# Reordering the first third of a three-layer CIN kernel: W1 and x of chunk 1 ahead of the pairs' x, chunk 5's right fields loaded, and one x1 product ahead of the A products

## The chip, the cores and the metric

One core of one Trainium2 chip. The metric is the device time of one execution in microseconds (us); the median of several runs is compared.

## What is computed

The reference applies three compressed-interaction layers to x, which has 64 samples, 32 fields and 64 embedding positions. Cut to what matters:

```python
X0 = inputs.reshape(-1, 32, 64)
Xi = X0
for W, b in ((W1, b1), (W2, b2), (W3, b3)):
    Wr = W.reshape(128, 32, Xi.shape[1])
    Xi = jnp.einsum('bhd,bmd,ohm->bod', X0, Xi, Wr) + b[None, :, None]
    pools.append(Xi.sum(axis=-1))
y = concatenate(pools, -1) @ fc_W.T + fc_b
```

Only a number for each sample is wanted of layers 2 and 3, so the kernel folds their weights with fc_W. What stays is one full product with W1 (called **x1**), one product of the same size with a small matrix **A** that the kernel itself works out from W3, W2 and fc_W, and their elementwise product, summed.

## The kernel before

**Tiling.** The 4096 columns (64 positions by 64 samples) are cut into 8 chunks of 512. The features of a chunk are products of a left and a right field: four 128-row tiles, in two halves of two tiles, and a small tile of 96 rows for pairs that the four do not hold. Each float32 factor is split in two parts, high and low (`xs`, `feat`, `w1_hi`/`w1_lo`, `a_hi`/`a_lo`), so that three fast matrix products replace an exact one.

**One chunk.** `split_x(c)`: ACT rounds x to the high part, POOL (L259) subtracts for the low part. `pick_right(c, half)` (L567): two PE matmuls select the right fields into PSUM. `mult(c, half)` (L461): DVE multiplies left by right. `hi(c, half)` (L366): ACT rounds. `lo(c)`: DVE (L484) subtracts for half 0, POOL (L266) for half 1. For chunks from `PICKED` (6) on, the right fields are not picked by PE but loaded as 1 MB by `load_right(c)` (L185) into `r_in`, and DVE multiplies two SBUF tiles. `x1_product(c)` is 13 PE matmuls (`x1_hi`, `x1_lo` for each half, then `x1_tail`) into one of two PSUM banks; ACT empties it by `save_x1(c)` (L372), and a product for chunk c waits for `save_x1(c - 2)`. `a_product(c)` is 14 matmuls of the same kind with A.

**The A chain.** `v_part(0..3)` (L639) multiply W3 by a window of fc_W into `vt_ps`; ACT copies it, PE transposes it (L700), ACT writes `v_st`. `a_round(0..3)` (L665) multiply that with W2; ACT empties each round by `save_a(t)` (L377) into `at_sb`; SP stores each round with three DMAs to a scratch tensor in HBM (L205), and once all twelve have landed (`a_out`) SP (L233, L237, L239) and ACT (L432) load them back, rearranged, into `f1` and `f2`. DVE adds the two (L530, L532; `f_sum`), ACT rounds to `a_hi`, DVE subtracts to `a_lo`. Only then can `a_product(0)` run.

**The pairs' tile.** `x16` is loaded (L385), multiplied (L514), split (`z16_hi` on ACT, `z16_lo` on POOL, L309), spread by PE (`spread16(0)`, `spread16(1)`, L652) and copied by ACT (`save_zz`) to `zz`, which `x1_tail` and `a_product` read.

**What sets the order.** Every engine runs one instruction stream in the order of the code, and semaphores order the engines among each other; the orders are written out by hand: SP from L208, POOL from L275, ACT from L385, DVE from L507, PE from L678. The loads stand in one SP queue: x 0, W1, x 1, W3 in four parts with x 2 between, x 3, W2 in four parts with x 4 between, the rest of W1, x 5, x 6. ACT's queue has only x16 and the small vectors. `keep_clock` (L562) issues matmuls whose result nobody reads. POOL's wait list is in order too: what stands behind `split_x(5)` waits until ACT has rounded x 5. Four lines show a coupling that the prediction uses; on ACT, behind A's twelve stores, stand the loads and then the next chunk:

```python
act.wait_ge(a_out, A_OUT)
for j in range(J):
    act.dma_start(f2[...], ...).then_inc(f_main_in, 16)
hi(5, 0); hi(5, 1)
```

Behind these are the copy to `v_rep` (L438), `save_x1(2)`, the wait for `f_sum`, `a_hi`, and `save_x1(3)` (L440 to L443).

## Time and profile before

| | before |
|---|---|
| median of 3 runs | 81.9 us (81.87 to 82.09) |
| the profiled execution | 81.76 us |
| its span | 80.0 us |
| mean granted TensorE clock | 0.998 |
| PE / PEld / DVE / ACT / POOL busy | 72.5 / 51.6 / 46.6 / 34.6 / 49.8 us |
| PE / POOL / ACT / DVE / DMA on the chain that ended last | 77% / 5% / 3% / 3% / 7% |
| moved by DMA | 12.01 MB |

The span is what lies between the first and the last instruction; 1.76 us of the execution lie around it. A busy share says how long an engine worked, not that the end waited for it; the chain of waits, followed back from the last instruction, says that. PEld is the loading of weights beside the matmuls. Times in the rows are microseconds from the span's start.

### The profile page before, as it was taken

Reading aid. Unit: us, or ns where it says so; the run is one execution under the profiler, and the core shown is the slowest. Engines: PE = TensorE matmul, PEld = TensorE weight load, DVE = VectorE, ACT = ScalarE, POOL = GpSimd, SP = SyncE. Lnnn points to the kernel's source line nnn. Section 1 sums busy time; section 2 is a strip of 40 time slices with the busy share of each in tenths; the row PEclk is TensorE's granted clock in tenths of the full one; section 3 lists DMA queues with packets and bytes.
Section 4 is the critical chain, followed back from the end, with each engine's and each line's share of the span. In section 5 each row is a group of like instructions: output and inputs, shape, how many; then the busy total and the mean of one; then the engine's idle time right before and its main releaser. Section 6 shows DMA issues by size and latency. Waiting matters only on the chain.

```text
span 80.0 us, 1146 instructions
## 1 busy us (share of the span) xinstructions
PE 72.5 (91%) x372; PEld 51.6 (65%) x372; DVE 46.6 (58%) x44; ACT 34.6 (43%) x51; POOL 49.8 (62%) x49
## 2 busy tenths in 40 slices
PE   4969499978999669999999999999999999999970
PEld 1315177843445356888888888888888888886840
DVE  1058699686859999289699819992003003213541
ACT  1833997279948956890864700552300300000000
POOL 4989846999994399738079989809955004162400
PEclk9999999999999999999999999999999999999999
DMA  1899999999995615439997000000000000000000
GB/s 22 250 362 266 368 370 351 381 386 390 372 330 163 189 37 135 117 69 381 394 335 307 12 4 0 4 0 0 0 0 0 0 0 0 0 8 0 0 0 0
DMA packets 7529, 12.01 MB, mean 150 GB/s; under 512 B 835, under 2 KB 3971, under 8 KB 7267
## 3 DMA queue, kind: packets, MB, share of 16 engines
q1 hardware_dynamic: 6915, 11.16, 40.8%
q10 hardware_dynamic: 608, 0.77, 3.1%
q8 instruction: 3, 0.05, 0.2%
q14 instruction: 3, 0.02, 0.1%
HBM read 10.88 MB, written 1.05 MB: 149 GB/s over the span
## 4 chain that ended last, share of the span: by engine, by line
PE 77%; DMA 7%; POOL 5%; ACT 3%; DVE 2%; issue 2%; SPq 1%; POOLq 0%; DVEq 0%
PE a_ps L581 28%; PE x_ps L581 25%; DMA w_sb<-w 7%; PE z_ps L575 6%; PE a_ps L674 5%; PE a_ps L636 2%; PE x_ps L609 2%; PE a_ps L635 2%; PE a_ps L647 2%; POOL w_sb L305 2%; POOL z_lo L309 2%; POOL xs L259 2%; DVE r_in L477 2%; PE a_ps L661 1%; PE x_ps L749 1%
## 5 line engine op out<-in xcount | busy, mean ns | idle before, releaser
L266 POOL TENSOR_TENSOR feat<-r_in,feat 128x1024 fp32r<-128x1024 f32 x8 | 19.2, 2403 | 4.6 <-ACT feat L360 4.1
L581 PE MATMUL x_ps<-feat,w_hi 128*128 128x512 f32 x64 | 19.0, 395 | 0.0
L581 PE MATMUL a_ps<-feat,a_hi 128*128 128x512 f32 x64 | 16.2, 395 | 0.0
L259 POOL TENSOR_TENSOR xs<-x_in,xs 32x512 fp32r<-32x512 f32 x7 | 10.8, 1548 | 7.6 <-ACT xs L360 7.3
L504 DVE SCALAR_TENSOR_TENSOR x<-a_ps,vec,x 128x512 f32<-128x512 f32 x7 | 5.2, 746 | 17.7 <-PE a_ps L636 17.7
L273 POOL TENSOR_TENSOR x<-x 128x512 f32<-128x512 f32 x6 | 7.8, 1292 | 10.7 <-DVE x L504 10.5
L581 PEld LDWEIGHTS x_ps<-feat,w_hi 128*128 128x128 f32 x64 | 11.9, 188 | 3.4 <-issue 0.8
L581 PEld LDWEIGHTS a_ps<-feat,a_hi 128*128 128x128 f32 x64 | 11.9, 188 | 2.7
L484 DVE TENSOR_TENSOR feat<-z_ps,feat 128x1024 fp32r<-128x1024 f32 x8 | 9.8, 1220 | 3.5 <-ACT feat L360 3.4
L360 ACT ACTIVATE feat<-z_ps 128x1024 fp32r<-128x1024 f32 x8 | 8.2, 1022 | 5.8 <-DVE z_ps L477 5.8
L581 PE MATMUL x_ps<-feat,w_lo 128*128 128x512 f32 x32 | 9.8, 391 | 0.0
L575 PE MATMUL z_ps<-xs,pick 128*128 128x512 f32 x24 | 7.6, 417 | 2.4 <-POOL xs L259 1.4
L374 ACT ACTIVATE x<-x_ps,vec 128x512 f32<-128x512 f32 x8 | 5.4, 682 | 9.5 <-PE x_ps L609 9.5
L360 ACT ACTIVATE feat<-r_in 128x1024 fp32r<-128x1024 f32 x8 | 8.4, 1055 | 2.2 <-DVE r_in L477 2.2
L581 PE MATMUL a_ps<-feat,a_lo 128*128 128x512 f32 x32 | 8.6, 390 | 0.0
L477 DVE TENSOR_TENSOR r_in<-x_in,z_ps 128x1024 f32<-128x1024 f32 x6 | 7.3, 1217 | 1.3 <-issue 1.3
L477 DVE TENSOR_TENSOR z_ps<-x_in,z_ps 128x1024 f32<-128x1024 f32 x6 | 7.4, 1226 | 1.2 <-PE z_ps L575 1.2
L575 PEld LDWEIGHTS z_ps<-xs,pick 128*128 128x128 f32 x24 | 4.0, 188 | 5.7 <-POOL xs L259 2.5
L581 PEld LDWEIGHTS x_ps<-feat,w_lo 128*128 128x128 f32 x32 | 6.0, 188 | 1.4
L581 PEld LDWEIGHTS a_ps<-feat,a_lo 128*128 128x128 f32 x32 | 6.0, 188 | 1.3
L565 PE MATMUL x_ps<-at_sb 128*128 128x512 bf16 x17 | 5.6, 494 | 1.2 <-DVE at_sb L507 1.2
L360 ACT ACTIVATE xs<-x_in 128x512 fp32r<-128x512 f32 x8 | 5.0, 628 | 2.6 <-DMA x_in<-xl 2.5
(76 smaller groups left out, 74.7 us busy)
## 6 DMA issues: line engine op xcount, KB each, us to landing
w_sb<-w SPq DMA_DIRECT2D x9, 512.0 KB, 8.7
x_in<-xl SPq DMA_DIRECT2D x8, 256.0 KB, 7.3
r_in<-xr SPq DMA_DIRECT2D x2, 1024.0 KB, 6.0
a_by_fields<-at_sb SPq DMA_DIRECT2D x8, 96.0 KB, 2.1
x<-x ACTq DMA_DIRECT2D x1, 512.0 KB, 4.5
x<-x SPq DMA_DIRECT2D x1, 512.0 KB, 6.2
w_sb<-w SPq DMA_DIRECT2D x1, 256.0 KB, 11.6
a_by_fields<-at_sb SPq DMA_DIRECT2D x4, 64.0 KB, 2.1
```

The lines of the kernel that those rows point to most:

```text
L259: nc.gpsimd.tensor_tensor(xs[rows, c, :], x_in[rows, c % X_BUFS, :], xs[rows, c, :].bitcast(f32), ALU.subtract).then_inc(xs_lo, 1)
L266: nc.gpsimd.tensor_tensor(feat[:, c, 1, of_half(1), :], z_of(c, 1), feat[:, c, 0, of_half(1), :].bitcast(f32), ALU.subtract).then_inc(lo_d ...
L273: nc.gpsimd.tensor_tensor(x1[:, 0, :], x1[:, 0, :], x1[:, c, :], ALU.add).then_inc(acc_done, 1)
L360: return nc.scalar.activation(dst, src, ACT.Copy)
L374: nc.scalar.activation(x1[:, c, :], x1_ps[c % 2][:, :], ACT.Identity, bias=vec[:, 0:1]).then_inc(x1_saved, 1)
L477: nc.vector.tensor_tensor(z_of(c, half), left, right, ALU.mult).then_inc(z_done, 1)
L484: nc.vector.tensor_tensor(feat[:, c, 1, of_half(0), :], z_of(c, 0), feat[:, c, 0, of_half(0), :].bitcast(f32), ALU.subtract).then_inc(lo_d ...
L504: nc.vector.scalar_tensor_tensor(out=x1[:, c, :], in0=a_ps[:, c % 2, :], scalar=vec[:, 3:4], in1=x1[:, c, :], op0=ALU.add, op1=ALU.mult).t ...
L565: nc.tensor.matmul(x1_ps[1][:, :], blank[:, 0:M], blank[:, 0:N], start=True, stop=True)
L575: last = nc.tensor.matmul(field_bank(c, half)[:, k, :], pick[:, half * PER_HALF + k, :], xs[:, c, :], start=True, stop=True)
L581: nc.tensor.matmul(bank, weights[:, k, :], feat[:, c, part, k, :], start=(start and k == 0), stop=False)
L674: last = nc.tensor.matmul(a_ps[64 * g:64 * g + 64, t % 2, :], v_st[:, :], w2_sb[:, first:first + N], start=True, stop=True)
```

## The change

- **Loads.** x16 leaves ACT's queue and stands in SP's behind W3's second part, so that nothing but x 0 stands before W1 and x 1. x 2, x 3 and x 4 each move one 512 KB part forward, W1's rest moves ahead of W2. `PICKED` is 5: chunk 5's right fields are loaded (`load_right(5)`, behind x 5) and `pick_right(5, ...)`, four matmuls, goes. The buffers of `r_in` go by `right_buf(c)`. `load_right(6)` and `load_right(7)` stand in SP's queue where those of 6 and 7 stood; that of 6 now waits for chunk 5's last use.
- **POOL.** W1's sum stands first, then `split_x(1)`; the small copies and `ident` come behind it; `lo(0)` moves ahead of `split_x(2)`; `z16_lo` moves behind `lo(1)`; the sum of W1's rest goes to DVE.
- **ACT.** `z16_hi` moves behind `hi(1, 1)`, the `v_st` copies behind `hi(2, 1)`, `save_zz(0)` behind them; the four `save_a` stand among `hi(3, 0)` to `hi(4, 1)`; `save_zz(1)` moves ahead of the wait for `a_out`.
- **DVE.** x16's product moves behind chunk 1, `rest_sum` stands between the two halves of chunk 3.
- **PE.** `spread16(0)` moves behind `pick_right(3, 0)`; all four `v_part`, both halves of `x1_hi(1)`, the transpose and the rounds of A take new places; `x1_product(5)` stands ahead of q and of the A products, `x1_product(6)` ahead of `a_product(2)`.

```diff
@@ -25,7 +25,7 @@
...
-PICKED = 6
+PICKED = 5
 X_BUFS = 4
@@ -129,6 +129,7 @@
...
         w_sum, w_hi_done, w_lo_done = sem("w_sum"), sem("w_hi_done"), sem("w_lo_done")
+        w_rest_sum = sem("w_rest_sum")
         f_sum, a_hi_done, a_lo_done = sem("f_sum"), sem("a_hi_done"), sem("a_lo_done")
@@ -164,13 +165,17 @@
...
+        def right_buf(c):
+
+            return (c - PICKED) % 2
+
         def z_of(c, half):
...
                 return r_in[:, 1, of_half(c % 2), :]
-            return r_in[:, c % 2, of_half(1), :]
+            return r_in[:, right_buf(c), of_half(1), :]
@@ -183,12 +188,12 @@
...
             def load_right(c):
-                if c % 2 == 0:
+                if c == PICKED:
                     sp.wait_ge(spread_done, 3)
                 else:
-                    sp.wait_ge(hi_done, count(PICKED - 1, 1))
-                    sp.wait_ge(lo_done[1], PICKED)
-                sp.dma_start(r_in[:, c % 2, :, :], xr[c]).then_inc(r_here[c % 2], 16)
+                    sp.wait_ge(hi_done, count(c - 1 if c == PICKED + 1 else c - 2, 1))
+                    sp.wait_ge(lo_done[1], c if c == PICKED + 1 else c - 1)
+                sp.dma_start(r_in[:, right_buf(c), :, :], xr[c]).then_inc(r_here[right_buf(c)], 16)
@@ -209,18 +214,20 @@
...
             load_w3(0)
+            load_x(2)
             load_w3(1)
-            load_x(2)
+            sp.dma_start(x16[:, :, :], bass.AP(x.tensor, 0, [[N, P], [HALF * COLS, 2], [1, N]])).then_inc(x16_in, 16)
+            load_x(3)
             load_w3(2)
             load_w3(3)
-            load_x(3)
+            sp.dma_start(w1_sb[:, :, EVEN:, :], w1[:, :, EVEN:, :]).then_inc(w1_rest_in, 16)
             load_w2(0)
+            load_x(4)
             load_w2(1)
-            load_x(4)
             load_w2(2)
             load_w2(3)
-            sp.dma_start(w1_sb[:, :, EVEN:, :], w1[:, :, EVEN:, :]).then_inc(w1_rest_in, 16)
             load_x(5)
+            load_right(PICKED)
             load_x(6)
@@ -238,12 +245,12 @@
...
                 scratch.tensor, FC2_COL * EXT * M, [[0, 3], [M, H], [1, M]])).then_inc(f_rest_in, 16)
-            load_right(PICKED)
+            load_right(PICKED + 1)
             sp.wait_ge(lo16_done, 1)
...
             load_x(7)
-            load_right(PICKED + 1)
+            load_right(PICKED + 2)
             sp.dma_start(fcb_sb[:, :], fc_b).then_inc(fcb_in, 16)
@@ -284,10 +291,6 @@
...
             nc.gpsimd.memset(ones[:, :], 1.0).then_inc(ones_done, 1)
-            nc.gpsimd.memset(ident[:, :], 0.0).then_inc(ident_done, 1)
-            pool.wait_ge(ident_done, 1)
-            nc.gpsimd.affine_select(out=ident[:, :], in_=ident[:, :], compare_op=ALU.not_equal, fill=1.0,
-                                    base=0, pattern=[[-1, P]], channel_multiplier=1).then_inc(ident_done, 1)
             pool.wait_ge(spread_done, 1)
@@ -296,37 +299,37 @@
...
             nc.gpsimd.tensor_copy(spread[:, :, :].rearrange("p t c -> p (t c)"), r_in[:, 0, 0, :]).then_inc(spread_done, 1)
+            pool.wait_ge(w1_in, 16)
+            nc.gpsimd.tensor_tensor(w1_sb[:, 0, 0:TILES, :], w1_sb[:, 0, 0:TILES, :], w1_sb[:, 1, 0:TILES, :],
+                                    ALU.add).then_inc(w_sum, 1)
+            pool.wait_ge(w_sum, 1)
+            pool.wait_ge(xs_lo, 1)
+            split_x(1)
+            pool.wait_ge(xs_lo, 2)
             pool.wait_ge(vec_in, 16)
...
             nc.gpsimd.tensor_copy(v_st[:, FC2_COL:FC2_COL + 1], vec[:, 4:5]).then_inc(fc2_done, 1)
-            nc.gpsimd.tensor_scalar(b23[:, :], vec[:, 1:3], float(D), 0.0, ALU.mult, ALU.add).then_inc(b23_done, 1)
-            pool.wait_ge(w1_in, 16)
-            nc.gpsimd.tensor_tensor(w1_sb[:, 0, 0:TILES, :], w1_sb[:, 0, 0:TILES, :], w1_sb[:, 1, 0:TILES, :],
-                                    ALU.add).then_inc(w_sum, 1)
-            pool.wait_ge(hi16_done, 1)
-            pool.wait_ge(w_sum, 1)
-            nc.gpsimd.tensor_tensor(z16_lo[:, :], x16[:, 0, :], z16_hi[:, :].bitcast(f32),
-                                    ALU.subtract).then_inc(lo16_done, 1)
-            pool.wait_ge(lo16_done, 1)
-            pool.wait_ge(xs_lo, 1)
-            split_x(1)
-            pool.wait_ge(xs_lo, 2)
+            nc.gpsimd.memset(ident[:, :], 0.0).then_inc(ident_done, 1)
+            pool.wait_ge(ident_done, 1)
+            nc.gpsimd.affine_select(out=ident[:, :], in_=ident[:, :], compare_op=ALU.not_equal, fill=1.0,
+                                    base=0, pattern=[[-1, P]], channel_multiplier=1).then_inc(ident_done, 1)
+            lo(0)
+            pool.wait_ge(lo_done[1], 1)
             split_x(2)
             pool.wait_ge(xs_lo, 3)
-            lo(0)
-            pool.wait_ge(lo_done[1], 1)
             split_x(3)
...
             pool.wait_ge(lo_done[1], 2)
+            pool.wait_ge(hi16_done, 1)
+            nc.gpsimd.tensor_tensor(z16_lo[:, :], x16[:, 0, :], z16_hi[:, :].bitcast(f32),
+                                    ALU.subtract).then_inc(lo16_done, 1)
+            pool.wait_ge(lo16_done, 1)
             split_x(4)
...
             lo(2)
-            pool.wait_ge(w1_rest_in, 16)
-            nc.gpsimd.tensor_tensor(w1_sb[:, 0, EVEN:, :], w1_sb[:, 0, EVEN:, :], w1_sb[:, 1, EVEN:, :],
-                                    ALU.add).then_inc(w_sum, 1)
-            pool.wait_ge(w_sum, 2)
+            pool.wait_ge(lo_done[1], 3)
             split_x(5)
@@ -334,8 +337,9 @@
...
             split_x(6)
+            pool.wait_ge(xs_lo, 7)
+            nc.gpsimd.tensor_scalar(b23[:, :], vec[:, 1:3], float(D), 0.0, ALU.mult, ALU.add).then_inc(b23_done, 1)
             pool.wait_ge(xp_in, 16)
-            pool.wait_ge(xs_lo, 7)
             xp = x16[:, :, :].rearrange("p g (d b) -> p (g d) b", b=B)
@@ -382,56 +386,55 @@
...
-            act.dma_start(x16[:, :, :], bass.AP(x.tensor, 0, [[N, P], [HALF * COLS, 2], [1, N]])).then_inc(x16_in, 16)
             act.dma_start(vec[:, :], vecs).then_inc(vec_in, 16)
...
             split_x(0)
-            act.wait_ge(z16_done, 1)
-            copy(z16_hi[:, :], x16[:, 0, :]).then_inc(hi16_done, 1)
             split_x(1)
...
             hi(0, 1)
-            save_zz(0)
             split_x(2)
...
             hi(1, 1)
+            act.wait_ge(z16_done, 1)
+            copy(z16_hi[:, :], x16[:, 0, :]).then_inc(hi16_done, 1)
             act.wait_ge(vt_ready, 1)
             copy(vt_sb[:, :], vt_ps).then_inc(vt_saved, 1)
+            hi(2, 0)
+            split_x(4)
+            hi(2, 1)
             act.wait_ge(v_ready, 1)
...
             copy(v_st[:, H + 8:H + 15], v_by_field[:, 1, 0:7]).then_inc(v_saved, 1)
-            hi(2, 0)
-            split_x(4)
-            hi(2, 1)
+            save_zz(0)
+            hi(3, 0)
+            act.wait_ge(w_rest_sum, 1)
+            copy(w1_hi[:, EVEN:, :], w1_sb[:, 0, EVEN:, :]).then_inc(w_hi_done, 1)
+            hi(3, 1)
             save_a(0)
+            split_x(5)
             save_a(1)
-            hi(3, 0)
+            hi(4, 0)
             save_a(2)
             save_a(3)
-            hi(3, 1)
-            act.wait_ge(w_sum, 2)
-            copy(w1_hi[:, EVEN:, :], w1_sb[:, 0, EVEN:, :]).then_inc(w_hi_done, 1)
-            split_x(5)
-            hi(4, 0)
             hi(4, 1)
...
             save_x1(1)
+            save_zz(1)
             act.wait_ge(zeros_done, ZEROS)
...
                     scratch.tensor, (TILES * j + k) * M, [[(EXT + 1) * M, H], [1, (TILES - k) * M]])).then_inc(f_main_in, 16)
-            save_zz(1)
             hi(5, 0)
@@ -468,8 +471,8 @@
...
                 else:
-                    dve.wait_ge(r_here[c % 2], 16)
-                    right = r_in[:, c % 2, tiles, :]
+                    dve.wait_ge(r_here[right_buf(c)], 16 * ((c - PICKED) // 2 + 1))
+                    right = r_in[:, right_buf(c), tiles, :]
                     if half == 0:
@@ -497,6 +500,12 @@
...
                                         main_hi[rows, EVEN:, :].bitcast(f32), ALU.subtract).then_inc(done, 1)
+
+            def rest_sum():
+
+                dve.wait_ge(w1_rest_in, 16)
+                nc.vector.tensor_tensor(w1_sb[:, 0, EVEN:, :], w1_sb[:, 0, EVEN:, :], w1_sb[:, 1, EVEN:, :],
+                                        ALU.add).then_inc(w_rest_sum, 1)
@@ -510,21 +519,22 @@
...
                                     ALU.subtract).then_inc(xs_lo, 1)
-            dve.wait_ge(x16_in, 16)
-            nc.vector.tensor_tensor(x16[:, 0, :], x16[:, 0, :], x16[:, 1, :], ALU.mult).then_inc(z16_done, 1)
             mult(0, 0)
...
             chunk(1)
+            dve.wait_ge(x16_in, 16)
+            nc.vector.tensor_tensor(x16[:, 0, :], x16[:, 0, :], x16[:, 1, :], ALU.mult).then_inc(z16_done, 1)
             chunk(2)
-            chunk(3)
-            mult(4, 0)
-            mult(4, 1)
+            mult(3, 0)
+            rest_sum()
+            mult(3, 1)
+            lo(3)
             dve.wait_ge(w_hi_done, 2)
             rest_lo(w1_sb[:, 0, :, :], w1_hi, w_lo_done)
-            lo(4)
+            chunk(4)
             chunk(5)
@@ -640,7 +650,6 @@
...
                     pe.wait_ge(window_done, 1)
-                    pe.wait_ge(zz_saved, 1)
                 pe.wait_ge(w3_in[n], 16)
@@ -654,6 +663,7 @@
...
                     pe.wait_ge(lo16_done, 1)
+                    pe.wait_ge(v_saved, 3)
                 else:
@@ -665,7 +675,7 @@
...
                 if t == 0:
-                    pe.wait_ge(v_saved, 3)
+                    pe.wait_ge(zz_saved, 1)
                     pe.wait_ge(fc2_done, 1)
@@ -680,54 +690,56 @@
...
             pick_right(0, 1)
-            keep_clock(6)
-            spread16(0)
+            keep_clock(8)
             x1_main(0, 0)
             pick_right(1, 0)
+            x1_main(0, 1)
             pick_right(1, 1)
-            x1_main(0, 1)
             x1_lo(0, 0)
+            v_part(0)
+            v_part(1)
             x1_low_weights(0, 0)
             x1_low_weights(0, 1)
-            v_part(0)
-            v_part(1)
+            x1_lo(0, 1)
+            pick_right(2, 0)
             v_part(2)
-            pick_right(2, 0)
+            v_part(3)
             pick_right(2, 1)
-            v_part(3)
+            x1_hi(1, 0)
+            x1_hi(1, 1)
             pe.wait_ge(ident_done, 2)
...
             nc.tensor.transpose(v_ps, vt_sb[:, :], ident[:, :]).then_inc(v_ready, 1)
-            x1_lo(0, 1)
+            x1_lo(1, 0)
             pick_right(3, 0)
+            spread16(0)
+            x1_lo(1, 1)
+            pick_right(3, 1)
             a_round(0)
             a_round(1)
-            x1_hi(1, 0)
-            pick_right(3, 1)
+            pick_right(4, 0)
+            pick_right(4, 1)
             a_round(2)
             a_round(3)
-            pick_right(4, 0)
-            x1_lo(1, 0)
-            pick_right(4, 1)
-            x1_hi(1, 1)
-            pick_right(5, 0)
-            x1_lo(1, 1)
             x1_tail(0)
             x1_tail(1)
-            pick_right(5, 1)
             spread16(1)
-            x1_product(2)
+            x1_hi(2, 0)
+            x1_lo(2, 0)
+            x1_hi(2, 1)
+            x1_lo(2, 1)
+            x1_tail(2)
             x1_product(3)
             x1_product(4)
+            x1_product(5)
             pe.wait_ge(v_saved, 4)
...
             a_product(1)
-            x1_product(5)
+            x1_product(6)
             a_product(2)
-            x1_product(6)
             a_product(3)
...
             for c in range(4, CHUNKS - 1):
```

## Rows read from the trace of the kernel before

**Rows 1.** The page: its head, and the busy time of PE.

```profile
span 80.0 us, 1146 instructions
...
PE 72.5 (91%) x372; PEld 51.6 (65%) x372; DVE 46.6 (58%) x44; ACT 34.6 (43%) x51; POOL 49.8 (62%) x49
```

**Rows 2.** The chain that ended last, in order of time: start, us, what.

```profile
9.64 0.44 PE a_ps L661
...
28.62 0.73 PE z_ps L575 x2
...
31.89 2.74 PE x_ps L581 x12
...
37.84 2.74 PE x_ps L581 x12
...
40.93 2.85 PE a_ps L581 x12
...
76.44 0.03 issue
```

**Rows 3.** DMAs issued from 0 to 2 us: count, KB each, median us to landing.

```profile
x_in<-xl SPq DMA_DIRECT2D x2, 256.0 KB, 4.6
x<-x ACTq DMA_DIRECT2D x1, 512.0 KB, 4.5
w_sb<-w SPq DMA_DIRECT2D x1, 512.0 KB, 5.5
```

**Rows 4.** The same for DMAs issued from 5.3 to 6.2 us (x of chunk 3).

```profile
x_in<-xl SPq DMA_DIRECT2D x1, 256.0 KB, 9.6
```

**Rows 5.** The same for DMAs issued from 8.5 to 12.2 us (x of chunk 4).

```profile
x_in<-xl SPq DMA_DIRECT2D x1, 256.0 KB, 8.8
```

**Rows 6.** The queue of SP in order of time: start, us, issues.

```profile
6.07 2.43 SPq L183 DMA_DIRECT2D x_in<-xl  x1
...
10.27 0.62 SPq L183 DMA_DIRECT2D x_in<-xl  x1
...
28.63 1.74 SPq L233 DMA_DIRECT2D f<-a_by_fields  x4
```

**Rows 7.** PE in order of time: start, us, line, what, idle before.

```profile
13.90 1.52 PE L647 MATMUL a_ps<-w_sb,window 128*32 128x128 f32 x48
...
19.33 1.94 PE L674 MATMUL a_ps<-w_sb,v_st 128*64 128x512 f32 x8
```

**Rows 8.** ACT and its queue in order of time.

```profile
20.54 0.61 ACT L360 ACTIVATE at_sb<-a_ps 128x512 f32<-128x512 f32 x1
...
24.77 0.60 ACT L360 ACTIVATE at_sb<-a_ps 128x512 f32<-128x512 f32 x1 [0.26 <-PE a_ps L674]
...
30.75 1.39 ACTq L432 DMA_DIRECT2D f<-a_by_fields  x3
...
33.11 1.01 ACT L360 ACTIVATE feat<-z_ps 128x1024 fp32r<-128x1024 f32 x1
34.01 1.06 ACT L360 ACTIVATE feat<-r_in 128x1024 fp32r<-128x1024 f32 x1
```

**Rows 9.** POOL in order of time.

```profile
6.80 1.28 POOL L305 TENSOR_TENSOR w_sb<-w_sb 128x512 f32<-128x512 f32 x1
...
35.21 2.40 POOL L266 TENSOR_TENSOR feat<-r_in,feat 128x1024 fp32r<-128x1024 f32 x1 [1.73 <-ACT feat L360]
...
43.01 3.45 POOL L345 TENSOR_TENSOR x<-x 128x512 f32<-128x512 f32 x3
```

**Rows 10.** DVE in order of time.

```profile
11.20 0.68 DVE L493 TENSOR_TENSOR w_lo<-w_sb,w_hi 128x512 fp32r<-128x512 f32 x1
11.80 1.23 DVE L477 TENSOR_TENSOR z_ps<-x_in,z_ps 128x1024 f32<-128x1024 f32 x1
...
35.40 2.77 DVE L530 TENSOR_TENSOR f<-f 128x512 f32<-128x512 f32 x1
```

**Rows 11.** The page: a DMA from issue to landing.

```profile
x<-x SPq DMA_DIRECT2D x1, 512.0 KB, 6.2
```

## The prediction

> **What bounds the kernel now.** The page comes first. Of a span of 80.0 us PE is busy 72.5 [rows 1], so PE is the bound on the average; the chain of waits in order of time then says where it is not. From 31.89 us, when `x1_product(2)` starts, to 76.44 us it is PE alone, matmul behind matmul: twelve take 2.74 us, 0.228 each [rows 2]. That stretch can't get shorter, it can only start sooner, or be broken. Ahead of it the chain walks over W1's landing, POOL and PE in turn, from `spread16(0)` at 9.64 on [rows 2]. Between 9.64 and 31.89 lie 22.25 us. The work of PE there is, counted in the code, 70 matmuls of 512 columns, of which 8 are the rounds of A [rows 7]: 70 x 0.232 = 16.2; the `v_part` matmuls, 16 in 0.48, 1.94 in all (48 took 1.52 with their tail, 1.45 without) [rows 7]; the transpose, 0.3. That is 18.5, so some 3.7 us are waiting. A change of order can gain at most that, and 4 picks less are 0.93.
>
> **The price of the start.** x16 (512 KB) lands 4.5 us after its issue at 0.74, at 5.2; W1 5.5 after its issue at 1.20 [rows 3], at 6.7, and POOL's sum starts at 6.80 [rows 9]. Two transfers of 512 KB thus land 1.5 us apart. Without x16 before it I put W1 at 5.3 and x 1 at 6.2 (bounds 5.0 and 6.8, the second where x16 was in nobody's way). Then POOL: sum 5.4 to 6.7 (1.28 [rows 9]), low part of x 1 to 8.1; ACT: `w1_hi` at 7.3; DVE: x 0 lands some 0.4 sooner, its products end at 7.6 and 8.8; ACT's `hi(0, 0)` 8.7. So `x1_main(0, 0)` starts at 8.85, where PE before began `spread16(0)` at 9.64 [rows 2]: 0.8 sooner. But PE catches up with what comes late anyway. From 8.85 it has 66 matmuls, the `v_part` and the transpose, 17.5 us; with no waits `x1_product(2)` would start at 26.4.
>
> **The waits that follow, one by one.** x 3 landed at 6.07 + 9.6 = 15.7 and x 4 at 10.27 + 8.8 = 19.1 [rows 4, 5, 6]. By the bytes ahead of them in SP's queue W3's last part now lands where x 3 did, at 15.7, and x 4 half a 512 KB part sooner, at 18.3 to 18.4. PE reaches `v_part(3)` at 14.8, waits 0.9, ends it at 16.2; with the second half of pick 2 and eight matmuls of `x1_hi(1)` the transpose ends at 18.8. ACT has `split_x(4)` from 18.3 to 18.9, then `hi(2, 1)` to 19.95 (1.06 [rows 8]), then the `v_st` copies to 20.25. `spread16(0)` waits for them: 20.4 to 21.3, PE idle 0.8. Then four matmuls, `save_zz(0)` to 22.4, and the first round of A starts at 22.6. Before it started at 19.33 [rows 7]: the A chain is now 3.3 late. That is the wait that takes the place of the ones removed. The rounds: `mult(3, 1)` ends at 23.8, `hi(3, 1)` at 24.9, `save_a(0)` 25.4, `split_x(5)`, `save_a(1)` 26.5, the last round of A 26.6 to 27.6, `hi(4, 0)` to 27.6 beside it, `save_a(2)` and `save_a(3)`, about 0.6 each [rows 8], to **28.65**. Call this moment S; before it was 25.37 [rows 8]. `spread16(1)` and `save_x1(0)` follow, and `x1_product(2)` starts at S + 1.65 = 30.3, 1.6 sooner than at 31.89.
>
> **The sum, from S on.** Before, the loads back of A (SP, 28.63) were issued 3.26 after S [rows 6, 8]. ACT waits for the same: its four DMAs, 0.46 each [rows 8], end at S + 5.1; `hi(5, 0)` and `hi(5, 1)`, 1.95 together [rows 8], at S + 7.05. POOL's `lo(5)` starts 0.14 later and takes 2.40; DVE's sum of f1 and f2 begins 0.19 later still and, where others of its shape take 0.68, took 2.77: it ended 0.56 after POOL did [rows 9, 10]. That order is fixed by the same three instructions, so I take it again: `f_sum` at S + 10.15. ACT writes `a_hi` and, behind it, `save_x1(3)`, both 0.6 and a handover: S + 11.6. `x1_product(5)`, now ahead of the A products, needs that bank. So `a_product(0)` starts at S + 11.6 + 2.97 + 0.12 = S + 14.7 = 43.35. Before it started at 40.93 [rows 2] with `x1_product(5)` still to come: 43.90 on the same work. The early part thus gives 0.55, of 1.6 that PE has at `x1_product(2)`: the waits in front of `x1_product(4)` (S + 8.2, behind `hi(5, 1)`, `v_rep` and `save_x1(2)`, against 30.3 + 5.95) and of `x1_product(5)` take 0.6 and 0.5.
>
> **Chunk 6.** `load_right(6)` waits for POOL's `lo(5)`: S + 9.7 = 38.35, where the load in its place was issued at 34.3. x for the sums goes out 0.45 later and lands 6.2 after [rows 11], S + 16.35. POOL folds it, 3.45 and 0.33 [rows 9] and gaps, then does `lo(6)`, 2.5: S + 22.8 = 51.45. PE wants it 2.3 into `x1_product(6)`, at 43.35 + 6.47 + 2.3 = 52.1. Covered by 0.65; one DVE product of two SBUF tiles in front of POOL's first fold (1.1) makes it 0.45 short. I book 0.2. The load of chunk 5's right fields, 1 MB more in the queue, lands by 27.5 at the pace of 512 KB in 1.4 to 1.5 us; its product begins at 28.9, so it costs nothing while that cover of 1.4 us stands. Its two products now read two SBUF tiles, and DVE takes them in turn with POOL's `lo(3)` and `lo(4)`: they end by 34.5 to 35.2, and ACT wants the second at 34.9. `rest_sum` on DVE costs 0.4 and frees 0.73 on POOL, both beside other work. `keep_clock` and the small POOL copies fill idle time. The granted clock is 0.998 over the run, and PE is idle before 31 us for under 1 us at a time as it was before (one gap of 1.4), so I price the clock at nothing (the rows show the upper of its two levels throughout).
>
> So 0.55 less 0.2, **0.35 us faster**: the profiled execution's 81.76 would be 81.4, and as the median of the runs stands 0.14 above it, I forecast 81.5.
>
> The Trainium skill has a rule that speaks against the change (SBUF — State Buffer, Who interferes with whom): a DVE instruction with two SBUF inputs and a GpSimd instruction that reads SBUF exclude each other for their whole length, whoever starts first. The f1 sum that ended 0.56 us after POOL agrees. Taken by itself, with every product at the length it has when nothing is beside it, the sum stays at 81.5; with the rule and the tie lost it is 82.9. By that rule every place where the change sets such a pair beside each other is a race, which is the first rival.
>
> **Rivals.** (1) **DVE blocked at `main_lo`**, slower. W1's low part (two SBUF tiles, 0.68 [rows 10]) would start at 9.95 to 10.0 on DVE, POOL's `lo(0)`, moved forward, at 10.0. If POOL is first, DVE waits 2.4 us, as L530 did, and `mult(1, 0)` moves from 10.5 to 12.95. For it: the tie, and L530 lost by 0.19. Against: DVE needs no semaphore from ACT there. Pushed on, `hi(2, 1)` ends 1.4 later; S comes at 30.0, `a_product(0)` at 44.7, and chunk 6 is short too: +0.8 and 0.2 to 0.4, **82.9**. It decides if POOL starts more than 0.05 us ahead. Chance 0.25; I put here also that other landings come late by the same amount. (2) **Given back**: `rest_sum` at 21.2 falls behind POOL's `lo(2)`, started at 20.75 in one order of the earlier pairs (behind it in the other), and delays `mult(3, 1)` by 0.85; S 29.3, `a_product(0)` 44.0, and chunk 6 between covered and 0.4 short: 0.1 to 0.5 slower than the forecast's zero, **82.1**. Chance 0.18. (3) **More than that**: x 4 lands 0.7 earlier and ACT runs `hi(2, 1)` right behind DVE; S 27.8, `a_product(0)` 42.5, which chunk 6 follows as it hangs on S as well: **80.6**. Chance 0.20. (4) **The change does not do what it says**: W1 lands at 6.7 still, since x16 was not what held it. For it: x16 was in another queue. The start is then 9.9, but S hangs on W3 and x 4, and PE has a wait of 0.9 at `v_part(3)` to lose: 81.6. It is another way to the forecast or to no change, and has 0.02.
>
> **How the numbers follow.** The forecast has 0.35. What a measurement of this kernel can tell from no change is 0.3%, 0.25 us. The forecast's own spread, S within 0.3 and chunk 6 from 0 to 0.45, is 81.1 to 81.9; I count 0.24 of it faster, 0.07 no change, 0.04 slower. Rival 1 is slower, 0.25. Rival 2 is split 0.11 no change and 0.06 slower, 0.01 faster. Rival 3 is faster, 0.20. Rival 4 is 0.02 no change. Faster 0.45, same 0.20, slower 0.35. The range takes in rival 3 and rival 1's middle: 80.5 to 82.9; half of rival 1 and a little of rival 3 lie outside.
>
> **What the profile of after should show.** W1's sum on POOL starts at 5.4 and PE's first x1 matmul at 8.85. The first round of A starts at 22.6 and the last `save_a` ends at 28.65, `x1_product(2)` at 30.3. In the chain there are two short waits, before `x1_product(4)` and before `x1_product(5)`, and the DVE row of the f1 sum takes about 2.8. `a_product(0)` starts at 43.4; if it starts 0.55 before 43.90 and nothing is short at chunk 6, the forecast is right. A `w_lo` row of about 3 us on DVE is rival 1; a `w_sb` row of over 2 us on DVE is rival 2; S before 28 is rival 3. The forecast is wrong above all if S is off: each 0.1 of it is 0.1 us of the end.

## The result and the profile after

| | before | after |
|---|---|---|
| median | 81.89 us (81.83 to 82.09, 4 runs) | 84.15 us (83.32 to 84.40, 4 runs) |
| ratio | 1 | 1.0256, 95% interval 1.0222 to 1.0291 |
| the profiled execution, span | 81.76, 80.0 | 84.34, 82.5 |
| last `save_a` ends (S) | 25.37 | 30.49 |
| `x1_product(2)` starts | 31.89 | 32.07 |
| q's matmul, ahead of `a_product(0)` | 40.65, and 43.6 with the 2.97 of `x1_product(5)` that now stand ahead of it | 45.45 |
| PE's stream ends | 76.44 | 79.04 |

The change is 2.6% slower. The forecast was 81.5 with a range of 80.5 to 82.9; sign and range were both wrong. The granted clock was 0.996 to 1.0 in the four executions, so the clock has no part in it. Ratios leave out executions that took over 1.5% longer than the fastest of their kernel, while medians and ranges take in all.

DVE of the changed kernel in order of time (start, us, line, what). L496 writes `w_lo`, L507 is `rest_sum`, L480 are chunk 5's two products of SBUF tiles, L540 is the sum of f1 and f2:

```profile
10.70 2.74 DVE L496 TENSOR_TENSOR w_lo<-w_sb,w_hi 128x512 fp32r<-128x512 f32 x1
13.36 1.22 DVE L480 TENSOR_TENSOR z_ps<-x_in,z_ps 128x1024 f32<-128x1024 f32 x1
...
22.71 0.72 DVE L507 TENSOR_TENSOR w_sb<-w_sb 128x256 f32<-128x256 f32 x1
...
30.79 1.83 DVE L480 TENSOR_TENSOR z_ps<-x_in,r_in 128x1024 f32<-128x1024 f32 x1
32.53 3.41 DVE L480 TENSOR_TENSOR r_in<-x_in,r_in 128x1024 f32<-128x1024 f32 x1
...
38.39 2.65 DVE L540 TENSOR_TENSOR f<-f 128x512 f32<-128x512 f32 x1
```

POOL of the same execution: W1's sum, `lo(0)`, the folds of the x for the sums, `lo(6)`:

```profile
6.61 1.27 POOL L303 TENSOR_TENSOR w_sb<-w_sb 128x512 f32<-128x512 f32 x1 [1.84 <-DMA w_sb<-w]
...
10.48 2.40 POOL L273 TENSOR_TENSOR feat<-r_in,feat 128x1024 fp32r<-128x1024 f32 x1 [0.22 <-ACT feat L364]
...
48.71 3.52 POOL L349 TENSOR_TENSOR x<-x 128x512 f32<-128x512 f32 x3 [3.09 <-DMA x<-x]
...
52.59 2.40 POOL L273 TENSOR_TENSOR feat<-r_in,feat 128x1024 fp32r<-128x1024 f32 x1
```

PE, only the rows with an idle time that matters (in brackets, with what ended it):

```profile
15.84 0.71 PE L585 MATMUL z_ps<-xs,pick 128*128 128x512 f32 x2 [0.64 <-DVE r_in L480]
...
22.17 0.44 PE L671 MATMUL a_ps<-z_hi,spread 128*96 128x512 f32 x1 [0.84 <-ACT v_st L364]
...
32.07 0.73 PE L591 MATMUL x_ps<-feat,w_hi 128*128 128x512 f32 x2 [0.35 <-ACT x L378]
...
38.80 0.74 PE L591 MATMUL x_ps<-feat,w_hi 128*128 128x512 f32 x2 [0.53 <-ACT x L378]
...
42.34 0.72 PE L591 MATMUL x_ps<-feat,w_hi 128*128 128x512 f32 x2 [0.26 <-ACT x L378]
...
55.04 0.73 PE L591 MATMUL x_ps<-feat,w_hi 128*128 128x512 f32 x2 [0.45 <-POOL feat L273]
```

Read together: POOL's `lo(0)` started at 10.48, DVE wanted `w_lo` at 10.70 and was done with it at 13.44, 0.56 us after POOL ended at 12.88. That is the row of before in which the f1 sum lost to `lo(5)` [rows 9, 10], in a new place. From there everything up to the last `save_a` is late. Then come the two short waits for `save_x1(2)` and `save_x1(3)`, and the wait for `lo(6)`. The stream ends 2.60 later than before: 1.8 of it is there at q (45.45 against 43.6), 0.7 more at the end of `x1_product(6)`, which took 3.7 us from its first matmul at 52.3 to the next product at 56.01, where an unbroken one takes 2.97.

The loads are a second reason for the late S. The first fence is ACT, with its `split_x` of chunk 1 and of chunk 4; the second is SP's issue of x 4 and the time that this load took from issue to landing:

```profile
7.25 0.63 ACT L364 ACTIVATE xs<-x_in 128x512 fp32r<-128x512 f32 x1 [2.89 <-DMA x_in<-xl]
...
20.23 0.62 ACT L364 ACTIVATE xs<-x_in 128x512 fp32r<-128x512 f32 x1
```

```profile
11.33 0.74 SPq L188 DMA_DIRECT2D x_in<-xl  x1
...
x_in<-xl SPq DMA_DIRECT2D x1, 256.0 KB, 8.5
```

x 1 was forecast to land at 6.2 and ACT could take it at 7.25. x 4 was forecast for 18.3 to 18.4 and landed at 19.8 (11.33 + 8.5). ACT took it at 20.23, behind `hi(2, 0)`, which the block of DVE had made late.

### The profile page after: what moved, and what is told of

Same layout as the page of the kernel before. It is cut to its first block, busy times and chain, and to the rows that moved or that the text cites. A ratio compares the mean times of both kernels' runs of the same rounds, so it can differ in the third digit from the quotient of the medians.

```text
span 82.5 us, 1140 instructions
## 1 busy us (share of the span) xinstructions
PE 73.9 (90%) x370; PEld 51.0 (62%) x370; DVE 52.2 (63%) x45; ACT 34.4 (42%) x51; POOL 49.0 (59%) x48
## 4 chain that ended last, share of the span: by engine, by line
PE 42%; DMA 16%; DVE 13%; POOL 12%; ACT 7%; issue 7%; SPq 1%; DVEq 0%; POOLq 0%
PE a_ps L591 20%; DMA x<-x 9%; DVE r_in L480 7%; DMA w_sb<-w 6%; PE x_ps L591 6%; ACT feat L364 6%; POOL feat L273 6%; DVE z_ps L480 5%; PE z_ps L585 4%; POOL x L349 4%; PE a_ps L684 2%; PE a_ps L646 2%; PE a_ps L645 2%; POOL w_sb L303 2%; PE a_ps L656 1%
## 5 line engine op out<-in xcount | busy, mean ns | idle before, releaser
L273 POOL TENSOR_TENSOR feat<-r_in,feat 128x1024 fp32r<-128x1024 f32 x8 | 20.4, 2556 | 6.1 <-ACT feat L364 5.8
L591 PE MATMUL x_ps<-feat,w_hi 128*128 128x512 f32 x64 | 19.6, 402 | 2.6 <-ACT x L378 1.1
L266 POOL TENSOR_TENSOR xs<-x_in,xs 32x512 fp32r<-32x512 f32 x7 | 10.1, 1438 | 7.9 <-ACT xs L364 7.6
L480 DVE TENSOR_TENSOR r_in<-x_in,r_in 128x1024 f32<-128x1024 f32 x3 | 8.1, 2686 | 0.0
L480 DVE TENSOR_TENSOR z_ps<-x_in,r_in 128x1024 f32<-128x1024 f32 x3 | 5.7, 1891 | 3.5 <-DMA r_in<-xr 3.5
L575 PE MATMUL x_ps<-at_sb 128*128 128x512 bf16 x19 | 6.6, 518 | 1.2 <-DVE at_sb L516 1.2
L585 PE MATMUL z_ps<-xs,pick 128*128 128x512 f32 x20 | 6.5, 423 | 0.6 <-DVE r_in L480 0.6
L480 DVE TENSOR_TENSOR z_ps<-x_in,z_ps 128x1024 f32<-128x1024 f32 x5 | 6.1, 1222 | 1.2 <-PE z_ps L585 1.2
L480 DVE TENSOR_TENSOR r_in<-x_in,z_ps 128x1024 f32<-128x1024 f32 x5 | 6.1, 1216 | 0.9 <-issue 0.9
```

What stands on the lines that cost most here:

```text
L266: nc.gpsimd.tensor_tensor(xs[rows, c, :], x_in[rows, c % X_BUFS, :], xs[rows, c, :].bitcast(f32), ALU.subtract).then_inc(xs_lo, 1)
L273: nc.gpsimd.tensor_tensor(feat[:, c, 1, of_half(1), :], z_of(c, 1), feat[:, c, 0, of_half(1), :].bitcast(f32), ALU.subtract).then_inc(lo_d ...
L480: nc.vector.tensor_tensor(z_of(c, half), left, right, ALU.mult).then_inc(z_done, 1)
L575: nc.tensor.matmul(x1_ps[1][:, :], blank[:, 0:M], blank[:, 0:N], start=True, stop=True)
L585: last = nc.tensor.matmul(field_bank(c, half)[:, k, :], pick[:, half * PER_HALF + k, :], xs[:, c, :], start=True, stop=True)
L591: nc.tensor.matmul(bank, weights[:, k, :], feat[:, c, part, k, :], start=(start and k == 0), stop=False)
```

## The experiments

Times are medians, with the lowest and highest; each kernel was compared with the kernel before on the same chip (81.85 to 81.88 there).

**1. One part of the change alone, in the kernel before**

```diff
             pool.wait_ge(xs_lo, 2)
+            lo(0)
+            pool.wait_ge(lo_done[1], 1)
             split_x(2)
             pool.wait_ge(xs_lo, 3)
-            lo(0)
-            pool.wait_ge(lo_done[1], 1)
             split_x(3)
```

> The kernel before with one part of the change alone: POOL's lo(0) moved ahead of split_x(2). Theory (DVE and POOL exclude each other when both read two SBUF tiles): POOL starts lo(0) at 11.05, DVE wants w_lo at 11.2 and gets it 0.56 us after POOL ends, so the w_lo row is 2.7 to 2.9 us instead of 0.68, mult(1, 0) starts near 13.9 instead of 11.8, and the time is 0.8 to 1.5 us over 81.9. Rival (the early order of POOL is harmless, PE waits for landings anyway): the row is long but the time is within 0.3 us of 81.9.

Measured: 83.15 (83.10 to 83.27), ratio 1.0161 (1.0145 to 1.0176). DVE in order of time:

```profile
11.26 2.79 DVE L493 TENSOR_TENSOR w_lo<-w_sb,w_hi 128x512 fp32r<-128x512 f32 x1
13.98 1.22 DVE L477 TENSOR_TENSOR z_ps<-x_in,z_ps 128x1024 f32<-128x1024 f32 x1
```

Against 11.20, 0.68 and 11.80 before [rows 10]. One swap of two POOL instructions costs 1.3 us, and `x1_product(2)` starts at 33.26 instead of 31.89. As the theory had it: this part of the change costs 1.3 us by itself, shown without the rest of it. No other single part was found to cost as much.

**2. The same collision taken out of the changed kernel**: POOL waits until DVE has written `w_lo`.

```diff
+            pool.wait_ge(w_lo_done, 1)
             lo(0)
             pool.wait_ge(lo_done[1], 1)
             split_x(2)
```

> The changed kernel, in which POOL's lo(0) also waits until DVE has written w_lo. Theory (DVE is blocked at main_lo, because POOL's lo(0) started 0.2 us ahead of it): the w_lo row of DVE falls from 2.74 to about 0.7 us, mult(1, 0) starts at 11.4 instead of 13.4, the last save_a ends about 1.0 us (0.6 to 1.4) before 30.5, and the run is that much faster than 84.15, about 83.2, if chunk 6 lets it. Rival (the late A rounds are set by the landing of W3 and x 4 and by the order on PE alone): the w_lo row is short but the last save_a moves by under 0.2 us and the time stays at 84.0 to 84.3.

Measured: five executions, 82.18, 82.54, 83.78, 83.86 and 83.90, all at the same clock; the ratio of 1.0061 (1.0035 to 1.0087) rests on the lower two, the profile is one of the upper three. DVE in it:

```profile
10.45 0.68 DVE L497 TENSOR_TENSOR w_lo<-w_sb,w_hi 128x512 fp32r<-128x512 f32 x1
...
22.08 2.53 DVE L508 TENSOR_TENSOR w_sb<-w_sb 128x256 f32<-128x256 f32 x1
```

The `w_lo` row is short and chunk 1's first product starts at 11.04, yet the last `save_a` ends at 30.68. The gain ran into the next collision: `rest_sum` now came 0.14 us after POOL's `lo(2)` (21.94) and took 2.53 us. In the changed kernel POOL was late and the same `rest_sum` took 0.72. Neither theory had this; the prediction's rival (2) had.

**3. Both collisions out**: the edit of experiment 2, and

```diff
+            pool.wait_ge(w_rest_sum, 1)
             lo(2)
             pool.wait_ge(lo_done[1], 3)
```

> As the run in which POOL's lo(0) waits for w_lo, and in the same way lo(2) waits until DVE has done rest_sum, which there took 2.53 us behind it. Theory (with the first collision gone the DVE product w1 rest falls into the next one, in most executions; that is why its times lay at two levels, 82.2 to 82.5 and 83.8 to 83.9): rest_sum takes 0.4 us, mult(3, 1) starts near 23.6 instead of 24.5, the last save_a ends near 29.8 instead of 30.7, and all executions lie near 82.3, with a spread of under 0.5. Rival (the two levels come from how W1 and x land, which differed from run to run by 1 us): rest_sum is short, but two levels stay.

Measured: 82.65 (82.55 to 83.26, 4 runs), ratio 1.0113 (1.0074 to 1.0152), 0.35 over what was expected. DVE and PE:

```profile
10.34 0.68 DVE L498 TENSOR_TENSOR w_lo<-w_sb,w_hi 128x512 fp32r<-128x512 f32 x1
...
21.91 0.42 DVE L509 TENSOR_TENSOR w_sb<-w_sb 128x256 f32<-128x256 f32 x1
```

```profile
31.08 0.73 PE L593 MATMUL x_ps<-feat,w_hi 128*128 128x512 f32 x2 [0.34 <-ACT x L380]
```

S is 29.51 and `x1_product(2)` starts 1.0 sooner than in the changed kernel. At the median this kernel is 1.5 under the changed kernel's 84.15. Not all of that belongs to the collisions: in the profiled executions 1.0 is there at q (44.45 against 45.45), and the rest is the wait inside `x1_product(6)`, which is absent here because x for the sums landed 5.6 us after its issue instead of 7.7, in the same order of loads. The upper level is gone, though one of four lies at 83.26, 0.7 over the lowest.

With both collisions out, S is still 0.86 later than the forecast's 28.65. ACT waits for x 4 here, and behind it stand `hi(2, 1)`, the `v_st` copies and the rounds of A:

```profile
19.24 0.64 ACT L366 ACTIVATE xs<-x_in 128x512 fp32r<-128x512 f32 x1 [0.84 <-DMA x_in<-xl]
```

Experiment 6 has the same wait (0.84, at 19.45) and an S of 29.73. So this part of the late S is the landing of x 4 and not a collision.

**4. ACT's order behind the A chain**

```diff
             hi(5, 0)
+            save_x1(2)
             hi(5, 1)
...
-            save_x1(2)
+            save_x1(3)
             act.wait_ge(f_sum, 1)
             copy(a_hi[:, 0:TILES, :], f1[:, 0:TILES, :]).then_inc(a_hi_done, 1)
-            save_x1(3)
```

> The changed kernel with ACT's save_x1(2) moved ahead of hi(5, 1) and save_x1(3) ahead of the wait for f_sum. Theory (ACT's order behind the late A chain breaks PE's stream twice, and the loads of chunk 6 bound the end after it): the waits before x1_product(4) and x1_product(5), 0.65 and 0.4 us, go, a_product(0) starts about 1.1 us sooner, near 44.6, but the wait inside x1_product(6) grows from 0.45 by as much, since it hangs on DMAs behind POOL's lo(5): 84.0 to 85, no gain. Rival (these two waits are lost time by themselves): 83.1.

Measured: 82.49, 83.66, 84.42 and 84.77, median 84.04, no gain at the median; they lie too far apart for a ratio. In the profiled execution, one of 82.49, the waits of 0.53 and 0.26 are gone and the one for `lo(6)` is there, larger:

```profile
53.27 0.73 PE L591 MATMUL x_ps<-feat,w_hi 128*128 128x512 f32 x2 [0.59 <-POOL feat L273]
```

The theory had it that what the two waits cost would be waited for again at chunk 6. This execution doesn't show that: it is 1.91 ahead of the changed kernel's at q (43.54 against 45.45) and still 1.77 ahead behind `x1_product(6)` (54.24 against 56.01). It keeps the lead because x for the sums landed 5.7 us after its issue and not 7.7. With 7.7 it would have taken about 84.5, an estimate from these rows that is near the two upper executions; they were not profiled. Four executions 2.3 us apart don't settle the size.

The edit did one thing more. `lo(5)` now stands behind `save_x1(2)` and starts after the sum of f1 and f2, which is no longer blocked; DVE's row is first, POOL's second:

```profile
37.79 0.68 DVE L540 TENSOR_TENSOR f<-f 128x512 f32<-128x512 f32 x1
```

```profile
38.18 2.54 POOL L273 TENSOR_TENSOR feat<-r_in,feat 128x1024 fp32r<-128x1024 f32 x1 [3.89 <-ACT feat L364]
```

So this experiment and those built on it take a third collision out as well. What that is worth alone was not tried.

**5. Chunk 6's loads freed**

```diff
-                    sp.wait_ge(hi_done, count(c - 1 if c == PICKED + 1 else c - 2, 1))
-                    sp.wait_ge(lo_done[1], c if c == PICKED + 1 else c - 1)
+                    sp.wait_ge(hi_done, count(c - 2, 1))
+                    sp.wait_ge(lo_done[1], c - 1)
...
-            load_right(PICKED + 1)
             sp.wait_ge(lo16_done, 1)
...
+            load_right(PICKED + 1)
```

> The changed kernel with load_right(6) waiting for chunk 4 instead of chunk 5 (its buffer was last used there), and the x of the sums issued ahead of it. Theory: the x of the sums lands near 44 instead of 48.6, POOL's folds are done by 49.5 instead of 52.6, lo(6) ends by about 53, the wait of 0.45 us inside x1_product(6) goes, and nothing else moves: 0.5 to 0.7 us faster than the changed kernel, 83.5. Rival (chunk 6's right fields, now landing later, hold DVE instead): the wait stays or grows.

Measured: 83.32 (82.98 to 83.58), ratio 1.0177 (1.0144 to 1.0210), 0.8 below the changed kernel. The x for the sums took 4.0 us from issue to landing, where the changed kernel, with a 1 MB load issued ahead of it, has 7.7 (and experiments 2, 3 and 4, with the same order, have 5.6 to 5.9), and POOL's folds start at 45.75 instead of 48.71:

```profile
45.75 4.37 POOL L349 TENSOR_TENSOR x<-x 128x512 f32<-128x512 f32 x3
```

The wait inside `x1_product(6)` is gone, those of ACT stay (0.51 and 0.25).

**6. All of it together**: the edits of experiments 3, 4 and 5.

> Both collisions removed, the two save_x1 moved forward, and chunk 6's loads freed: all waits that the theory names, together. Theory: x1_product(2) starts near 31.4 and PE then has no wait to the end, a_product(0) starts near 43.4 and the time is 81.4 (81.2 to 82.0), a little under the kernel before. Rival (something not named, such as chunk 5's products of two SBUF tiles on DVE, holds the stream once these are gone): over 82.2, with a new wait ahead of x1_product(5) or inside it.

Measured: 82.05 (81.49 to 82.46, 10 runs), ratio 1.0017 (0.9988 to 1.0046). The chain that ended last, in order of time:

```profile
31.30 3.02 PE x_ps L593 x12
34.32 0.23 PE x_ps L621
...
40.50 2.74 PE x_ps L593 x12
43.24 0.24 PE x_ps L621
43.48 0.12 PE a_ps L739 x2
43.60 2.85 PE a_ps L593 x12
```

From 31.3 on PE has no wait that counts. The profiled execution took 81.50, as expected; the median is 0.6 above it. All named waits together are 2.1 of 84.15, which brings the change back to the kernel before and no further.

**7. Chunk 5 picked again**: the edits of 3 and 4, and

```diff
-PICKED = 5
+PICKED = 6
...
+            pick_right(5, 0)
             x1_tail(0)
             x1_tail(1)
             spread16(1)
+            pick_right(5, 1)
```

with chunk 6's right fields loaded behind x 5.

> Both collisions removed and the two save_x1 moved forward; chunk 5's right fields are picked by PE again (four matmuls, 0.93 us, half of them behind the last A round) and chunk 6's stand in the load queue where chunk 5's stood. Theory (loading chunk 5 costs DVE: its two products took 5.2 us where picked ones take 2.4, and made chunk 6's load late): DVE's products of chunk 5 end about 2.5 us sooner, PE pays 0.93 less what it waits for anyway, 0.5 or so, and the time is 82.0, within 0.5 of the run with the same changes and chunk 5 loaded. Rival (four picks less are a plain gain of 0.93): 0.9 slower than that run.

Measured: 81.89 (81.51 to 82.26, 10 runs), ratio 1.0002 (0.9983 to 1.0020). Chunk 5's products end at 32.2 instead of 35.2 (as in experiment 6):

```profile
29.34 1.22 DVE L481 TENSOR_TENSOR z_ps<-x_in,z_ps 128x1024 f32<-128x1024 f32 x1
31.01 1.22 DVE L481 TENSOR_TENSOR r_in<-x_in,z_ps 128x1024 f32<-128x1024 f32 x1 [0.45 <-PE z_ps L586]
```

```profile
52.61 0.73 PE L592 MATMUL x_ps<-feat,w_hi 128*128 128x512 f32 x2 [0.81 <-POOL feat L272]
```

The second fence is PE: this kernel still waits 0.81 for `lo(6)`, and is level with experiment 6 all the same. The four picks saved by loading chunk 5 are thus not a plain gain of 0.93.

**8. The transpose early**: experiment 6, and

```diff
             pick_right(2, 1)
-            x1_hi(1, 0)
-            x1_hi(1, 1)
             pe.wait_ge(ident_done, 2)
             pe.wait_ge(vt_saved, 1)
             nc.tensor.transpose(v_ps, vt_sb[:, :], ident[:, :]).then_inc(v_ready, 1)
+            x1_hi(1, 0)
+            x1_hi(1, 1)
             x1_lo(1, 0)
```

with the `v_st` copies on ACT ahead of `hi(2, 0)`.

> As the run with all waits removed, and the transpose and the v_st copies moved ahead of x1_hi(1, 0) and hi(2, 0). Theory (A's rounds are late because the transpose stands behind eight matmuls and its copies behind hi(2, 1)): spread16(0) starts 0.5 to 0.8 us sooner, the last save_a 0.5 sooner, and the time falls by 0.3 to 0.5 us against that run, to about 81.0. Rival (hi(2, 0) and hi(2, 1), now later, hold lo(2) and chunk 3): no gain or up to 0.3 slower.

Measured: 81.40 (80.91 to 82.53, 8 runs), ratio 0.9931 (0.9906 to 0.9957) without the two upper ones (82.25 and 82.53): the fastest kernel of the study, 0.5 us under the kernel before and 0.65 under experiment 6 at the median. PE:

```profile
20.74 0.44 PE L673 MATMUL a_ps<-z_hi,spread 128*96 128x512 f32 x1 [0.23 <-issue]
...
30.64 0.73 PE L593 MATMUL x_ps<-feat,w_hi 128*128 128x512 f32 x2 [0.35 <-ACT x L380]
```

`spread16(0)` starts at 20.74 instead of 21.40, `x1_product(2)` at 30.64 instead of 31.30. Of these 0.66 only 0.33 reach the end of the profiled execution (81.17 against 81.50): PE now comes to chunk 6 sooner than its features are ready. The chain there runs over chunk 6's right fields, which landed 6.1 us after their issue, to the last matmuls of `x1_product(6)`:

```profile
38.96 6.12 DMA r_in<-xr
...
51.91 0.74 PE x_ps L593 x2
```

**9. x16 back in ACT's queue**, in the kernel of experiment 8

```diff
+            act.dma_start(x16[:, :, :], bass.AP(x.tensor, 0, [[N, P], [HALF * COLS, 2], [1, N]])).then_inc(x16_in, 16)
             act.dma_start(vec[:, :], vecs).then_inc(vec_in, 16)
```

> The fastest run so far (all waits removed, transpose early) with x16's load back at the head of ACT's queue; all other loads keep their new order. Theory (x16 in its own queue held W1 at 6.7 in every execution; without it W1 lands anywhere from 5.5 to 6.6, which is the spread of 1 to 1.6 us of all kernels that have it in SP's queue): W1's sum starts at 6.8 as before, x1_product(2) starts 0.1 to 0.4 later than 30.64, the median is 81.5 to 81.9, and the spread of the times is under 0.4 us. Rival (the spread comes from later loads or from the races of DVE and POOL that are left): W1's sum starts at 6.8 and the spread stays over 1 us.

Measured: 82.49 (82.07 to 82.96, 7 runs), ratio 1.0081 (1.0055 to 1.0107). W1's sum starts at 6.84, where experiment 8 has 6.08, and `x1_product(2)` at 31.51 instead of 30.64:

```profile
6.84 1.27 POOL L302 TENSOR_TENSOR w_sb<-w_sb 128x512 f32<-128x512 f32 x1 [2.09 <-DMA w_sb<-w]
```

So taking x16 out of ACT's queue, the first thing that the change does, is a real gain: 1.1 us at the median, where undoing it was expected to cost 0.1 to 0.5. It works through x 1 more than through W1. ACT takes x 1 at 8.13 here and at 7.25 in experiment 8, 0.88 apart, which is what `x1_product(2)` loses. W1's sum ends, in both, before ACT is done with x 1.

```profile
8.13 0.63 ACT L365 ACTIVATE xs<-x_in 128x512 fp32r<-128x512 f32 x1 [3.43 <-DMA x_in<-xl]
```

The other 0.8 by which the profiled executions differ are a longer wait for `lo(6)` (0.73 idle). The spread fell from 1.6 to 0.9 us, not under 0.4: W1's landing is at most a part of it.

**10. `x1_product(5)` back behind `a_product(1)`**, in the kernel of experiment 8

```diff
             x1_product(4)
-            x1_product(5)
...
             a_product(1)
-            x1_product(6)
+            x1_product(5)
             a_product(2)
+            x1_product(6)
```

> The fastest run so far (all waits removed, transpose early) with x1_product(5) back behind a_product(1) and x1_product(6) behind a_product(2). Theory (A comes 4 us later than before, a_lo is ready at 42.0 and 42.6): PE would reach a_product(0) near 39.8 and waits some 0.5 to 1.2 us for a_lo inside it, which nothing gives back, since chunk 6 is then no longer the later one: 0.4 to 1.0 us slower than that run, 81.8 to 82.4. Rival (the order of the products is indifferent once chunk 5's and 6's features are in time): within 0.2 us of 81.4.

Measured: 82.22 (81.54 to 82.57, 5 runs), ratio 1.0066 (1.0042 to 1.0090). PE has two new waits, for `a_lo` inside `a_product(0)` and for DVE's product ahead of a later A product:

```profile
41.85 1.20 PE L593 MATMUL a_ps<-feat,a_lo 128*128 128x512 f32 x4 [0.16 <-DVE a_lo L498]
...
49.97 0.50 PE L593 MATMUL a_ps<-feat,a_hi 128*128 128x512 f32 x1 [0.25 <-DVE x L515]
```

The order of the change is the better one here, by 0.8 at the median; the idle time of the two waits, 0.4, is half of that. The profiled executions are only 0.37 apart.

## Why the prediction was wrong

- **The step that failed** is S, the end of the last `save_a`, in "The waits that follow, one by one": it was put at 28.65 and was 30.49. Two terms ahead of it were wrong.
- **The first is the order at `main_lo`.** The forecast rests on DVE reaching it first, at "9.95 to 10.0 on DVE, POOL's `lo(0)` ... at 10.0". POOL was ahead by 0.22. A tie that costs VectorE up to 2.4 us when it is lost was taken at its good side, and given 0.25 on the bad one; in all four profiles in which `lo(0)` is moved forward and not held (the changed kernel, experiments 1, 4 and 5) POOL was first, by 0.06 to 0.22. With this and the collision it hid taken out, S is 1.0 sooner (experiment 3). Rival (1) named the mechanism and its place. It had S at 30.0 and 82.9; alone in the kernel before, the collision costs 1.3.
- **The second is the landing of the loads.** x 4 was put at 18.3 to 18.4 "By the bytes ahead of them in SP's queue" and landed at 19.8; in the nine profiles with x16 in SP's queue it landed at 18.5 to 19.8, each later than forecast. It is why S stays at 29.51 and 29.73 with both collisions out (experiments 3 and 6). No rival had it on this side: rival (3) had x 4 still earlier, and rival (1) took in "other landings" only by its chance.
- **Rival (2)**, `rest_sum` behind `lo(2)`, was right as a mechanism and waits behind rival (1): it shows once the first is mended (2.53 us in experiment 2).
- **From S to `a_product(0)` the sum nearly held.** It had `x1_product(5)` at S + 11.6, which is 42.1: measured 42.34. Put 1.84 later, it has `a_product(0)` at 45.2; measured 45.6. The two waits for ACT were forecast at 0.6 and 0.5 and came at 0.53 and 0.26 of idle time in the rows; the f1 sum took 2.65 where 2.77 was booked.
- **"Chunk 6" was under-priced.** 0.2 was booked, 0.7 measured. The x for the sums was taken at its old 6.2 us from issue to landing and took 7.7 in the profiled execution. Both 1 MB loads were now issued within 1.4 us around it, at 40.57 and 41.98, where before the second came 2.9 behind it. That is not enough to explain it: experiments 2, 3 and 4 have the same 1.4 us, and there it took 5.9, 5.6 and 5.7. What made it 2 us longer in this execution stays open. Issued ahead of the 1 MB load it takes 4.0 (experiment 5), and the run is 0.8 faster.
- **The price of the start** was too good. W1 was put at 5.3 and its sum started at 6.61; in the other kernels with x16 in SP's queue it started at 5.51 to 6.22. What sets the start is x 1, put at 6.2 and taken at 6.77 to 7.25 in these nine profiles, so PE's first x1 matmul came at 9.60 and not at 8.85. Yet the start is worth more than the prediction let it be ("PE catches up with what comes late anyway"): 1.1 us (experiment 9).
- **Right**: the A chain as the wait that takes the place of the others, 3.3 late by forecast at the first round of A, 5.1 measured (24.46 against 19.33). Of the 1.8 over the forecast 1.0 is gone in experiment 3, where the first round starts at 23.48, and 0.8 is the late x 4. Right too were the load of chunk 5's right fields as no loss of its own (experiments 6 and 7 are 0.16 apart) and the clock.

Left open is the spread. The kernel before lies within 0.3 us, also with the one swap of experiment 1 (0.17); every kernel with the change's loads spreads over 0.6 to 2.3 us. Experiment 9 takes part of that away. One candidate is in the profiles: the same 512 KB load in the same order took 5.6 to 7.7 us to land, and its landing sets when POOL can begin the folds ahead of `lo(6)`. Each kernel has one profile only, so that this makes the spread is not shown.

## What to carry to other kernels

When a change moves an elementwise instruction of GpSimd, list the VectorE instructions with two SBUF operands that may start within a microsecond of it, and order each such pair by a semaphore so that the short one goes first: a wait of 0.6 us is cheaper than a block of 2.4. When a chain hangs on a load, give its landing the error that the profiles show (here 1.3 us between kernels with the same bytes ahead of it), and not one value from the bytes. Where two engines arrive within the accuracy of the estimate, the bad side belongs in the forecast, not beside it. And mend the waits one behind the other: here the first removed wait showed the next, and only all of them together brought the time back to that of the kernel before.

## What the hardware showed that was not expected

A VectorE instruction of 0.68 us became one of 2.74 to 2.88 behind a GpSimd instruction of 2.40 that had started 0.06 to 0.22 us sooner, and ended 0.54 to 0.56 us after it, in each of six rows (`w_lo` in four profiles, the sum of f1 and f2 in the kernel before and in experiment 1). Queued alternately, two products that take 1.22 us each with one operand in PSUM took 1.83 and 3.41 with both in SBUF, while GpSimd's two subtractions beside them took 5.72 instead of 4.83. The Trainium skill states it as a rule (SBUF — State Buffer, Who interferes with whom: issue order decides who blocks); the runs agree, and add the price of a lost tie in a kernel bound by TensorE: 1.3 us.

With a load of 512 KB in ACT's queue W1's, the second in SP's, landed late: its sum started at 6.80 to 6.84 in each of the three profiles with it; without it, W1's sum started at 5.51, 5.67, 5.69, 5.73, 5.82, 6.08, 6.18, 6.22 and 6.61 in nine profiles. The mean gained 0.87 us and the landing became uncertain by 1.1.
